# Second retention, feed-forward and expert layer in two lanes of two sequences

## The reference, cut to what matters

```python
def _L1_attn_ref(x):                       # the 4 sequences play the part of time (l = 4)
    h = layernorm(x, ln1_w, ln1_b)         # x here is already normalised once
    h = silu(h_prev * conv_w[:, 0] + h * conv_w[:, 1])     # h_prev: the sequence before
    q, k, v, g = silu(h @ Wq), h @ Wk, h @ Wv, h @ Wg
    q, k = rope(q), rope(k)
    scores = softmax(einsum(v, router_w))  # two routes for each head, the larger is taken
    ...                                    # masked_scores, masked_indices, norm_score
    qk = einsum(q_exp, k_exp) * HDK ** -0.5 * causal       # sequence l looks at m <= l
    o = per_head_norm(qk @ v)
    attn_out = (silu(g) * o) @ Wout + residual
    h2 = layernorm(attn_out, ln2_w, ln2_b)
    return silu(h2 @ w1) * (h2 @ w3) @ w2 + attn_out
def _L1_ffn_ref(x):                        # 8 experts, hidden width 512
    comb = top2(softmax(x @ router_w.T))
    h = gelu(einsum('nc,ech->enh', x, w1))
    return einsum('ne,enc->nc', comb, einsum('enh,ehc->enc', h, w2))
```

## Time and profile before

| | us |
|---|---|
| median of 3 runs | 321.98 |
| the profiled execution, its time | 322.6 |
| its span, first to last instruction | 320.5 |
| PE busy in the span | 252.0 (79%) |
| DVE busy | 183.8 (57%) |
| ACT busy | 121.5 (38%) |
| POOL busy | 40.5 (13%) |
| mean granted clock of TensorE, as a share of full speed | 0.903 |

### The profile page before, as it was taken

One profiled execution on the slowest core, in us unless ns is written; L12 is line 12 of the kernel. 1 busy time (PEld: TensorE's weight loads), 2 busy tenths in 40 slices (PEclk: granted clock), 3 DMA queues, 4 the chain that ended last, 5 costly groups with the idle time before them and its releaser, 6 DMA issues.

```text
span 320.5 us, 4776 instructions
## 1 busy us (share of the span) xinstructions
PE 252.0 (79%) x1860; PEld 166.8 (52%) x1860; DVE 183.8 (57%) x488; ACT 121.5 (38%) x251; POOL 40.5 (13%) x48
## 2 busy tenths in 40 slices
PE   8889668767759888699995786861048899999995
PEld 8346446546424574234672555730045656767775
DVE  6573688867446769998644566747944452111112
ACT  1443669733260105333207767104033163333220
POOL 4000000000200018266210000115003010000000
PEclk9975999977795999999999999967559999999999
DMA  7950000002960120000000000000000000000000
GB/s 230 304 191 0 3 1 2 2 2 66 429 292 0 49 85 2 0 0 0 0 2 2 2 0 2 4 0 1 0 0 0 2 1 0 3 0 0 2 0 33
DMA packets 5387, 13.73 MB, mean 43 GB/s; under 512 B 2161, under 2 KB 3313, under 8 KB 4722
## 3 DMA queue, kind: packets, MB, share of 16 engines
q1 hardware_dynamic: 4064, 10.73, 9.2%
q10 hardware_dynamic: 1298, 2.66, 2.6%
HBM read 13.13 MB, written 0.26 MB: 42 GB/s over the span
## 4 chain that ended last, share of the span: by engine, by line
PE 34%; DVE 11%; ACT 6%; POOL 2%; issue 1%; DVEq 0%; POOLq 0%
PE BK L1803 12%; PE BK L1816 9%; ACT WTF L787 4%; PE BK L1980 2%; PE BK L1993 2%; PE BK L1845 2%; POOL RSTD L568 2%; PE BK L1894 1%; PE BK L1904 1%; DVE STAT L867 1%; PE BK L1997 1%; DVE MX L1331 1%; PE BK L1503 1%; DVE XH L891 1%; PE BK L1889 1%
## 5 line engine op out<-in xcount | busy, mean ns | idle before, releaser
L1803 PE MATMUL BK<-XT,WTF 128*128 128x512 f32 x128 | 58.2, 596 | 0.9 <-DVE WTF L1280 0.8
L1803 PEld LDWEIGHTS BK<-XT,WTF 128*128 128x128 f32 x128 | 23.4, 190 | 27.2 <-issue 23.5
L568 POOL TENSOR_TENSOR RSTD<-VE,MHALF 128x2 f32<-128x2 f32 x14 | 9.6, 702 | 194.7 <-DVE VE L882 153.4
L1297 DVE SCALAR_TENSOR_TENSOR X<-BK,CW,X 128x128 f32<-128x128 f32 x32 | 9.0, 344 | 43.8 <-PE BK L1816 43.8
L1816 PEld LDWEIGHTS BK<-WTF 128*128 128x128 f32 x256 | 29.7, 192 | 3.3 <-issue 3.3
L1816 PE MATMUL BK<-WTF 128*128 128x128 f32 x256 | 29.7, 275 | 0.0
L773 ACT ACTIVATE WTF<-BK 128x512 f32<-128x512 f32 x32 | 18.8, 597 | 28.8 <-PE BK L1803 28.8
L707 ACT ACTIVATE WTF<-BK 128x512 f32<-128x512 f32 x40 | 22.5, 601 | 7.8 <-PE BK L1605 7.7
L1063 DVE TENSOR_SCALAR WTF<-WTF 128x512 f32<-128x512 f32 x40 | 16.8, 422 | 12.2 <-ACT WTF L707 11.8
L1515 PE MATMUL BK<-ident 128*128 128x128 f32 x160 | 21.4, 295 | 0.3 <-DVE SM L1039 0.3
L1515 PEld LDWEIGHTS BK<-ident 128*128 128x128 f32 x160 | 20.6, 211 | 0.9 <-DVE SM L1039 0.6
(11 more groups left out here) (257 smaller groups left out, 420.9 us busy)
## 6 DMA issues: line engine op xcount, KB each, us to landing
WTF<-w_f_dram SPq DMA_DIRECT2D x2, 2048.0 KB, 15.0
WTF<-w_c_dram SPq DMA_DIRECT2D x1, 2048.0 KB, 7.8
decay<-c_decay_dram ACTq DMA_DIRECT2D x1, 1024.0 KB, 7.2
decay<-mask_q_dram SPq DMA_DIRECT2D x1, 1024.0 KB, 4.9
crows_sb<-c_rows_dram ACTq DMA_DIRECT2D x1, 544.0 KB, 8.0
w_e_sb<-w_e_dram SPq DMA_DIRECT2D x1, 480.0 KB, 3.8
w_b_sb<-w_b_dram SPq DMA_DIRECT2D x1, 384.0 KB, 4.8
WTF<-win_dram SPq DMA_DIRECT2D x1, 320.0 KB, 4.2
```

The costliest lines, as they stand in the source:

```text
L568: pool.tensor_tensor(RSTD[:, pair], VE[:, pair], MHALF[:, pair], ALU.pow).then_inc(ln_rstd, 1)
L1803: ins = pe.matmul(hbank(u), w1[:, o:o + P], XT[:, :], start=True, stop=True)
```

## The change

Sequences 0 and 1 are lane 0, sequences 2 and 3 lane 1. Every step of stages E and F is done for one lane at a time (256 columns in place of 512, 2 matmuls in place of 4), and lane h has the PSUM banks 4h to 4h + 3 for itself. Lane 0 goes through retention and feed-forward alone. After that the steps of lane 1's retention and feed-forward stand between lane 0's experts in the queues of PE, ACT, DVE and POOL, and lane 1's experts come last. Silu and the softmax over two routes are written with Tanh, so that DVE multiplies by (1 + tanh) (`gated_xT`, `gated_q`, `gate_out`, `gated_ff`, `shares`), with factors of 1/2 put into constants. X is stored with one DMA for each lane.

The diff, cut to the queues' order and the functions that matter here:

```diff
+        lane_bank = lambda h, i: bank(4 * h + i)
+        lane_cols = lambda h: slice(256 * h, 256 * h + 256)
+        lane_pair = lambda h: slice(2 * h, 2 * h + 2)
...
+                    def rotate(h):
+                        pair = lane_pair(h)
+                        qk, qr, q2 = flat(QK[:, pair]), flat(QR[:, pair]), flat(Q2[:, pair])
+                        pool.wait_ge(l_q, h + 1)
+                        settle(pool.tensor_tensor(qr, qk, cs[:, 0, pair], ALU.mult))
+                        for b in range(2):
+                            for f in range(2):
+                                settle(pool.tensor_tensor(halves(q2)[:, b, :, f, :], halves(qk)[:, b, :, 1 - f, :],
+                                                          halves(cs[:, 1, pair])[:, b, :, f, :], ALU.mult))
+                        pool.tensor_tensor(qr, qr, q2, ALU.add).then_inc(l_rot, 1)
...
+                    lane_power(LN_E, 0)
+                    rotate(0)
+                    lane_power(LN_E2, 0)
+                    lane_power(LN_E, 1)
+                    bypass(0)
+                    lane_power(LN_F, 0)
+                    rotate(1)
+                    lane_power(LN_E2, 1)
+                    bypass(1)
+                    lane_power(LN_F, 1)
...
+                    def take_qkvg(h):
+                        pair = lane_pair(h)
+                        qkvg = BK[:, 4 * h + 1:4 * h + 3, :]
+                        act.wait_ge(l_qkv_ps, h + 1)
+                        act.activation(QK[:, pair].rearrange("p b a n -> p b (a n)"), qkvg[:, :, 0:128], ACT.Copy).then_inc(l_qkv, 1)
+                        act.activation(TQ[:, pair, :], qkvg[:, :, 0:64], ACT.Tanh, scale=0.5).then_inc(l_qkv, 1)
+                        act.activation(LGT[:, :, pair, :].rearrange("p r b h -> p b r h"),
+                                       qkvg[:, :, WE_R:WE_G].rearrange("p b (r h) -> p b r h", r=2), ACT.Copy).then_inc(l_qkv, 1)
+                        act.activation(VV[:, pair, :], qkvg[:, :, 128:256], ACT.Copy).then_inc(l_qkv, 1)
+                        act.activation(GS[:, pair, :], qkvg[:, :, WE_G:WE_O], ACT.Copy).then_inc(l_qkv, 1)
+                        act.activation(TG[:, pair, :], qkvg[:, :, WE_G:WE_O], ACT.Tanh, scale=0.5).then_inc(l_qkv, 1)
...
+                    def deviation(h):
+                        act.wait_ge(l_vs, h + 1)
+                        act.activation(SM2[:, lane_pair(h), :], SM1[:, lane_pair(h), :], ACT.Sqrt, bias=col("eps4"), scale=4.0 / HD)\
+                           .then_inc(std_ready, 1)
...
+                    def gelu(h, e):
+                        if e >= 2:
+                            act.wait_ge(e_y_ps, NE * h + e - 1)
+                        for p in range(2):
+                            act.wait_ge(e_h_ps, before_f + 2 * NE * h + 2 * e + p + 1)
+                            act.activation(GT[:, e % 2, 2 * p:2 * p + 2, lane_cols(h)],
+                                           lane_bank(h, 2 + p).rearrange("p (a n) -> p a n", a=2), ACT.Gelu).then_inc(e_act, 1)
...
+                    gate_xT(1)
+                    route(0)
+                    gelu(0, 0)
+                    take_qkvg(1)
+                    gelu(0, 1)
+                    between(1)
+                    square(1)
+                    deviation(1)
+                    gelu(0, 2)
+                    context(1)
+                    gelu(0, 3)
+                    second_xT(1)
+                    gelu(0, 4)
+                    gate_ff(1, (0, 1))
+                    gelu(0, 5)
+                    gate_ff(1, (2,))
+                    gelu(0, 6)
+                    gelu(0, 7)
+                    last_xT(1)
+                    route(1)
+                    for e in range(NE):
+                        gelu(1, e)
 
...
-                    def weigh(e):
-                        dve.wait_ge(e_y_ps, e + 1)
-                        if e:
-                            dve.wait_ge(e_sum, 2 * e)
-                        for b in range(B):
-                            ins = dve.scalar_tensor_tensor(out=X[:, b, :], in0=BK[:, 4 + e % 2, b * P:(b + 1) * P],
-                                                           scalar=CW[:, b, e:e + 1], in1=X[:, b, :],
-                                                           op0=ALU.mult, op1=ALU.add)
-                            if b % 2:
-                                ins.then_inc(e_sum, 1)
...
+                    def gated_q(h):
+                        q = QK[:, lane_pair(h), 0, :]
+                        dve.wait_ge(l_qkv, 6 * h + 2)
+                        dve.scalar_tensor_tensor(out=q, in0=TQ[:, lane_pair(h), :], scalar=1.0, in1=q,
+                                                 op0=ALU.add, op1=ALU.mult).then_inc(l_q, 1)
...
+                    def weigh(h, e):
+                        dve.wait_ge(e_y_ps, NE * h + e + 1)
+                        if e:
+                            dve.wait_ge(e_sum, NE * h + e)
+                        for i in range(2):
+                            b = 2 * h + i
+                            ins = dve.scalar_tensor_tensor(out=X[:, b, :], in0=lane_bank(h, e % 2)[:, i * P:(i + 1) * P],
+                                                           scalar=CW[:, b, e:e + 1], in1=X[:, b, :], op0=ALU.mult, op1=ALU.add)
+                        ins.then_inc(e_sum, 1)
...
+                    lane_norm(LN_E, 1, X)
+                    gated_ff(0)
+                    finished(0)
+                    convolve(1)
+                    lane_norm(LN_F, 0, X)
+                    gated_xT(1)
+                    chances(0)
+                    best_two(0)
+                    gated_q(1)
+                    choices(1)
+                    shares(1)
+                    gate_out(1)
+                    weights(1)
+                    weigh(0, 0)
+                    outputs(1)
+                    centred(1)
+                    bypass(1)
+                    variances(1)
+                    weigh(0, 1)
+                    contexts(1)
+                    weigh(0, 2)
+                    attended(1)
+                    weigh(0, 3)
+                    lane_norm(LN_E2, 1, CT)
+                    weigh(0, 4)
+                    gated_ff(1, (0, 1))
+                    weigh(0, 5)
+                    gated_ff(1, (2,))
+                    finished(1)
+                    weigh(0, 6)
+                    lane_norm(LN_F, 1, X)
+                    weigh(0, 7)
+                    chances(1)
+                    best_two(1)
+                    for e in range(NE):
+                        weigh(1, e)
 
...
-                    def down(e):
-                        if e >= 2:
-                            pe.wait_ge(e_sum, 2 * e - 2)
-                        for b in range(B):
-                            for j in range(4):
-                                if b == 0:
-                                    pe.wait_ge(e_act, before_f + 4 * e + j + 1)
-                                w = w_f2[:, (4 * e + j) * D:(4 * e + j + 1) * D]
-                                ins = pe.matmul(BK[:, 4 + e % 2, b * P:(b + 1) * P], GT[:, e % 2, j, b * P:(b + 1) * P], w,
-                                                start=(j == 0), stop=(j == 3))
-                        ins.then_inc(e_y_ps, 1)
 
...
+                    def up(h, e):
+                        for p in range(2):
+                            if e:
+                                pe.wait_ge(e_act, before_f + 2 * NE * h + 2 * e + p - 1)
+                            for i in range(2):
+                                o = (4 * e + 2 * p + i) * P
+                                ins = pe.matmul(lane_bank(h, 2 + p)[:, 256 * i:256 * i + 256], w_f1[:, o:o + P], XT[:, lane_cols(h)],
+                                                start=True, stop=True)
+                            ins.then_inc(e_h_ps, 1)
+                    def down(h, e):
+                        if e == 0:
+                            pe.wait_ge(r_z, 2 + h)
+                        if e >= 2:
+                            pe.wait_ge(e_sum, NE * h + e - 1)
+                        for i in range(2):
+                            b = 2 * h + i
+                            for j in range(4):
+                                if i == 0 and j % 2 == 0:
+                                    pe.wait_ge(e_act, before_f + 2 * NE * h + 2 * e + j // 2 + 1)
+                                w = w_f2[:, (4 * e + j) * D:(4 * e + j + 1) * D]
+                                ins = pe.matmul(lane_bank(h, e % 2)[:, i * P:(i + 1) * P], GT[:, e % 2, j, b * P:(b + 1) * P], w,
+                                                start=(j == 0), stop=(j == 3))
+                        ins.then_inc(e_y_ps, 1)
                     stay_warm(3)
-                    norm_T(LN_E, 7)
...
+                    lane_norm_T(LN_E2, 0, 1)
+                    lane_norm_T(LN_E, 1, 0)
+                    ff_up(0)
...
+                    logits(0)
+                    pe.wait_ge(loads["w_f1"], 16)
```

(30 more changed lines are left out.)

715 lines of the change are left out of this document (408 added, 307 removed).

## The result

The changed kernel took 332.74 us (median of 4 runs, 329.23 to 335.19) where the kernel before took 321.66 (321.11 to 325.84, 4 runs): the ratio is 1.028, with a 95% interval of 1.014 to 1.042. The forecast was 332.8. On another chip the same kernel had medians of 332.78 against 324.75, with a ratio of the means of all runs of 1.031 (1.018 to 1.045; 5 runs against 6). The clock granted in the early stages differs from execution to execution, so the runs spread (316.33 to 326.21 us for the kernel before on the second chip), and against its one run at 316.33, the four lower runs of the change, mean 332.31, are 5% longer. So it is slower, by 1.4 to 4.5% by the two intervals; whether it is over 2% the first interval alone does not settle, the second nearly does.

The account below looks back on a forecast made before the run. Stage E was seen as a relay with PE idle during DVE's retention, the experts as PE-bound. From 321.98 us, -16.0 + 7.6 + 0.3 + 7.4 + 8.45 + 3.0 = +10.8 gave 332.8 us; range 325 to 340.

Parts of the forecast that it names:

- Lead-in: Stage E up to the first expert, now for lane 0 alone, gets shorter: -16.0 us.
- Lane 1's work on PE: Lane 1's steps (+7.6) and slightly longer expert ups (+0.3) add 7.9 us on PE without cover.
- The stall at the context: PE idles 7.4 us before lane 1's context transposes: a chain of 14.5 against 7.05 us of lane 0's experts.
- POOL's rotation with its waits 4.7: In lane 1's chain to the context, the rotation on GpSimd was counted as 4.7 us before the weights.
- The table load: ScalarE's load of 1.28 us, counted within Square, table load and Sqrt (2.1 us) in the chain to the context.
- Queue order: Among lane 0's experts, PE's next step needs something begun only after its last step: stalls summing to 8.45 us.
- Clock: TensorE at half rate after the context stall loses 2.2 us, and lane 0's cold `stay_warm` 0.8: +3.0 us.
- 2.2 more for two of the later stalls: Upper bound of the clock cost: two later stalls also lower the clock, at 2.2 us more each, +7.4 in all.
- The first: Rival: within 2%, 325.8 us, with GpSimd's rotation at its lower bound in both lanes and no further clock fall; 16%.
- The third: Rival: each short stall lowers the clock and lane 0's last experts run at 1.2 GHz, 337 to 340 us; 10%.
- The second: Rival: faster, 313.9 us, as PE's 7.05 us cover lane 1's retention and the ordered stalls are absorbed; 5%.
- The fourth: Rival: each table switch adds a pause of ACT behind its load, 1.4 us each for two more, 335.6 us; 1%.

Follow-up runs that it names:

- e10_no_rotation: The changed kernel without lane 1's rotation on GpSimd except one small signalling instruction; PE's wait for lane 1's context is 1.23 us shorter.
- e2_short: The changed kernel with only lane 1's steps behind its context transposes moved later among lane 0's experts; median 318.6 us (314.94 to 322.20).
- e6_late_warm: The e1_late kernel plus useless matmuls filling PE's two waits in lane 0's lead-in; median 317.24 us, runs from 308.67 to 323.55.
- e1_late: The changed kernel with lane 1's steps, context transposes included, moved later among lane 0's experts; median 314.34 us against 324.68 for the kernel before.
- e5_rotation: The changed kernel without the four small products of lane 1's rotation on GpSimd; PE's wait for lane 1's context 6.68 us against 6.90.
- e8_warm_27: The changed kernel with 27 useless matmuls ahead of lane 1's context transposes; median 329.60 us against 332.78, ratio 0.991 (0.979 to 1.004).
- e7_serial: The changed kernel with all of lane 1's steps behind lane 0's last expert; first up product to end 101.8 us, 17.5 more than the changed kernel.

## Why the prediction was right

The forecast of 332.8 us agrees with the median of 332.74, and by its own steps mostly for its own reasons; but the agreement is closer than the terms deserve. Against the profiled execution the sum was 3.9 us too high (+10.8 where the spans differ by 6.9), and the median made up for it because the other executions had a lower granted clock (0.882 to 0.902 against 0.911). That part of the agreement is luck.

- **Lead-in, -16.0.** It was -17.3, and stage E began 0.4 earlier. To the projections 6.0 us (6.5 predicted), projections 3.10 (2.9), retention 11.2 (11.8), context 2.4 (2.1), to the feed-forward 5.5 (6.1), feed-forward with its sum 5.8 (5.7), to the first expert 4.3 (4.4). No piece off by more than 0.6.
- **Lane 1's work on PE, 7.9.** 7.5.
- **The stall at the context, 7.4.** 6.90, in every profile of these orders 6.89 to 6.91. The chain was 13.9 us (246.45 to 260.37) and not 14.5, the cover 7.0.
- **Inside that chain a step failed.** "POOL's rotation with its waits 4.7" is not what the weights wait for. VectorE is busy for 3.9 us there, 2.7 with GpSimd quiet (`e10_no_rotation`), and GpSimd is done 0.5 us before it; the rotation's part is the 1.2 us that it takes from VectorE. My reason for the middle value, "DVE and POOL hold each other up", was the right mechanism, put into the wrong term. (The upper bound was summed wrongly, too: two at 0.88 and four at 0.70 are 1.7 more than the middle value, not 1.9; measured were 0.73, 0.80 and four in 1.69.) The table load, taken whole, counts for 0.3 to 0.7 of its 1.28. q took 1.0 and not 0.8. The weights, `weigh(0, 0)`, products, sums, centring, Square to Sqrt and the last 0.8 are as predicted to 0.1 us.
- **Queue order, 8.45.** 7.32: 0.37 (0.7 predicted), 1.22 (1.4), 1.14 (1.3), 1.48 (1.65), 1.22 and 0.47 (2.0), 1.42 (1.4). All seven at the places named (the list has six steps, not five), each ended by the engine named. `e2_short` shows the cause: moving the steps one or two places takes 6.5 us of them away. "They are there even if DVE were twice as fast" was not tested.
- **Clock, 3.0.** 1.9 behind the long wait (2.2 predicted). In lane 0 the cold `stay_warm` took 4.74 us and not 3.07, but lane 1's transposes waited for their data behind it anyway (0.55 us); with the clock up, context to first expert was 0.8 us shorter in `e6_late_warm`, as predicted. The upper bound, "2.2 more for two of the later stalls", nearly came true in the kernel's second profile, with one stretch and not two: 86.55 us against 84.32.
- **Rivals.** The first falls in both halves: the rotation's length was not what counted, and the clock fell in both profiles of this kernel. The third's 337 to 340 us came once in nine runs of this kernel (338.97, clock 0.868). The second put its condition rightly, a chain of 7.05 us against one of 13.9, but missed its other side: the cover need not stay at 7.05 us. In `e1_late` it is 14, with the chain unchanged. The fourth falls: the Sqrt starts at 259.15, 0.01 us behind its load.

## What to carry to other kernels

When one lane's serial work is put between another's, compare the chain with the work that stands in the queue ahead of its first consumer, and place the consumer there: here 13.9 us of chain stood behind 7.0 us of cover, and two more experts ahead of it were worth 7.3 us at no cost. Then look at every later step whose input can only be made after the queue's last instruction: here such neighbours cost 0.4 to 1.5 us each, and most of them nothing one or two places later. Here a change that was 3% slower became a gain of 2 to 3% in another order.

## What was not expected of the hardware

- An instruction of VectorE on 32 elements took 0.73 us beside a GpSimd product of 256 elements, and 0.20 us without it (`e10_no_rotation`). Two in a row were held up where two large products of GpSimd stood in a row (`e5_rotation`).
- Waits of 1.2 us in pairs brought the clock to half in some executions and not in others with the same waits: no stretch at half behind the short waits in the first profile of the kernel after, one in its second, two in `e8_warm_27`. In `e6_late_warm` it fell behind waits at which it held in `e1_late`. What decides that is open.
- Halving a retention on VectorE does not halve it: 11.2 us for the lane with 3 pairs and 13.9 for the one with 7, against 18.2 for all 10 in one go. The sum of both is 25.1. Lane 1's 13.9 has two weighings of lane 0 in it and 1.2 of GpSimd's hold; with no weighing beside it, in `e7_serial`, it took 13.4.
